# Count-matrix builder of a graph network: one-hots stored with the eight items in the last dimension, and ScalarE fetching slot numbers four at a time

## The reference

```python
def gin_conv(x, W, b, src, dst):
    agg = jax.ops.segment_sum(x[src], dst, num_segments=N)
    return (x + agg) @ W + b
```

## Time and profile before

| | us |
|---|---|
| median of 3 runs | 10942.0 |
| lowest and highest run | 10923.65, 10950.61 |
| the profiled execution | 10955.16 |
| its span | 10953.4 |
| the stage `count_pairs` in it, first DVE step to last ACT step | 3632.6 to 5558.7 |

### The profile page before, as it was taken

How to read it: one execution, slowest core, us unless ns; L and a number is a source line. 1 busy time by engine, 2 the same in 40 slices (tenths; PEclk the granted TensorE clock), 3 DMA queues, 4 the chain that set the end, 5 groups by cost and what they waited for, 6 DMA issues and landing times. The chain is left out here.

```text
span 10953.4 us, 166923 instructions
## 1 busy us (share of the span) xinstructions
PE 6082.3 (56%) x43186; PEld 5047.6 (46%) x43187; DVE 5266.2 (48%) x9074; ACT 2226.6 (20%) x4530; POOL 3602.8 (33%) x3345
## 2 busy tenths in 40 slices
PE   0123333333331556665147766777778778877696
PEld 0122333333331211111046766677777777777496
DVE  6666333333331799998133455233333333333344
ACT  0464000000000344444410000111111111111132
POOL 0001777777776000000000000344545545444100
PEclk9999999999999756665577888788898989898697
DMA  0200222222221222222154755222222222222263
GB/s 21 100 0 9 40 41 41 40 40 40 41 41 26 42 52 52 52 52 52 51 213 159 280 219 213 79 75 73 77 75 75 76 74 76 75 75 74 39 221 119
DMA packets 1450866, 876.35 MB, mean 80 GB/s; under 512 B 905023, under 2 KB 1376596, under 8 KB 1425535
## 3 DMA queue, kind: packets, MB, share of 16 engines
q1 hardware_dynamic: 1237570, 639.77, 20.4%
q0 software_dynamic: 106048, 137.48, 6.0%
q10 hardware_dynamic: 107136, 97.57, 2.5%
HBM read 713.06 MB, written 159.27 MB: 80 GB/s over the span
## 5 line engine op out<-in xcount | busy, mean ns | idle before, releaser
L653 POOL DMA_INDIRECT out_records<-scatter_recs,scatter_rows x1650 | 1958.9, 1187 | 1194.7 <-issue 1194.1
L1567 POOL DMA_INDIRECT edge_mlp_b_rows<-b_table,edge_mlp_recs x1664 | 1633.5, 982 | 2130.7 <-DMA edge_mlp_recs<-out_records 1626.1
L712 PE MATMUL scatter_sum<-scatter_attr,scatter_hot 128*128 128x65 f32 x3328 | 810.5, 422 | 1503.3 <-DMA scatter_attr<-in_edge_attr 1258.2
L712 PEld LDWEIGHTS scatter_sum<-scatter_attr,scatter_hot 128*128 128x128 f32 x3328 | 741.2, 328 | 1572.7 <-DMA scatter_attr<-in_edge_attr 1131.6
L1027 PE MATMUL pairs_p_ring<-pairs_hot_near,pairs_hot_far 128*128 128x512 f16 x2256 | 956.5, 575 | 726.2 <-ACT pairs_p_ring L1046 635.1
L1010 DVE TENSOR_TENSOR pairs_hot_near<-c_iota_wide,pairs_shift 128x4096 f16<-128x4096 f16 x282 | 1244.8, 4414 | 0.0
L1682 DVE CAST edge_mlp_hot_t<-edge_mlp_p_hot 128x512 f32<-128x512 bf16 x416 | 287.6, 691 | 1844.7 <-PE edge_mlp_p_hot L1611 1307.9
L1027 PEld LDWEIGHTS pairs_p_ring<-pairs_hot_near,pairs_hot_far 128*128 128x128 bf16 x2256 | 276.3, 122 | 1406.0 <-issue 1370.7
L760 DVE TENSOR_TENSOR nodes_wide_sums<-nodes_wide_sums,scatter_sum 128x65 f32 x1664 | 384.8, 231 | 1008.2 <-issue 857.2
L1621 PE MATMUL edge_mlp_p_pre<-edge_mlp_hot_t,edge_mlp_a_blk 128*128 128x128 f32 x3328 | 726.5, 303 | 197.8 <-DVE edge_mlp_hot_t L1682 145.6
L1104 POOL MEMSET sum_x_parts<- 128x192 bf16 x2 | 0.5, 260 | 2444.1 <-POOLq L123 2444.1
(11 more groups left out here) (419 smaller groups left out, 9559.0 us busy)
## 6 DMA issues: line engine op xcount, KB each, us to landing
sum_x_tiles<-edge_counts SPq DMA_DIRECT2D x78, 1536.0 KB, 7.6
edge_mlp_a_blk<-a_table SPq DMA_DIRECT2D x1664, 64.0 KB
edge_counts<-pairs_cells ACTq DMA_DIRECT2D x744, 128.0 KB, 1.7
sum_z_tiles<-edge_counts SPq DMA_DIRECT2D x48, 1920.0 KB, 7.8
sum_y_tiles<-edge_counts SPq DMA_DIRECT2D x39, 1536.0 KB, 7.7
scatter_attr<-in_edge_attr SPq DMA_DIRECT2D x1664, 32.0 KB
sum_x_tiles<-edge_counts SPq DMA_DIRECT2D x26, 1664.0 KB, 9.9
pairs_ends<-out_records SPq DMA_DIRECT2D x2256, 1.0 KB, 1.6
```

The lines of the kernel that those rows point to most:

```text
L653: pool.indirect_dma_start(out=out_rec, out_offset=bass.IndirectOffsetOnAxis(ap=rows[s][:, c:c + 1], axis=0), in_=recs[s][:, c], in_offset= ...
L712: mm = pe.matmul(psum[s][:, c, 0:F + 1], hot[s][:, c], attr[s][:, c], start=True, stop=True)
L1567: pool.indirect_dma_start(out=b_rows[s][:, c], out_offset=None, in_=b_tab, in_offset=bass.IndirectOffsetOnAxis(ap=recs[s][:, c, FE + 1:FE ...
```

## The change

The two constant rows are made eight times as long, each number standing eight times in a row. The one-hots are laid out with the eight items innermost: `hot_far[s]` is now `[P, P, BATCH]`, `hot_near[s]` `[P, SUPER, BATCH]`. The comparisons read the long constant row as it lies, and on the other side the eight numbers of the batch again and again, with step 1 within the eight. The number for `hot_far` gets a small bf16 buffer of its own, `low`, with an instruction that fills it; both comparisons stand behind a wait for `shift` and `low`. PE reads item `c` of a batch as `[:, :, c]`, so that neighbouring columns of both operands lie 8 elements (16 bytes) apart. ACT fetches `until`, `plane` and `cell` for four slots at a time.

```diff
-            nc.gpsimd.iota(k["iota_b"][:], [[1, P]], base=0, channel_multiplier=0,
+            nc.gpsimd.iota(k["iota_b"][:], [[1, P], [0, BATCH]], base=0, channel_multiplier=0,
...
-            nc.gpsimd.iota(k["iota_wide"][:], [[1, SUPER]], base=0, channel_multiplier=0,
+            nc.gpsimd.iota(k["iota_wide"][:], [[1, SUPER], [0, BATCH]], base=0, channel_multiplier=0,
...
-        hot_far = [sb(f"hot_far{s}", [P, BATCH, P], BF16) for s in range(BATCHES)]
-        hot_near = [sb(f"hot_near{s}", [P, BATCH, SUPER], FP16) for s in range(BATCHES)]
+        low = [sb(f"low{s}", [P, BATCH], BF16) for s in range(BATCHES)]
+        hot_far = [sb(f"hot_far{s}", [P, P, BATCH], BF16) for s in range(BATCHES)]
+        hot_near = [sb(f"hot_near{s}", [P, SUPER, BATCH], FP16) for s in range(BATCHES)]
...
+        def slots_row(engine, name, it, s, low, top, why):
+            _, values = nc.values_load_multi_w_load_instructions(
+                rows[name][0:1, ds(it * RING + s, HALF)], engines=[engine], min_val=low, max_val=top,
+                skip_runtime_bounds_check_because=why)
+            return values
...
-                    low = ends[s][:].bitcast(BF16)[:, :, 1]
-                    dve.tensor_tensor(hot_far[s][:], bc(k["iota_b"][:], 1, BATCH), bc(low, 2, P),
+                    dve.tensor_copy(low[s][:], ends[s][:, :, 0]).then_inc(shifted[s], 1)
+                    dve.wait_ge(shifted[s], it * 2 + 2)
+                    dve.tensor_tensor(hot_far[s][:], k["iota_b"][:], bc(low[s][:], 1, P),
                                       ALU.is_equal).then_inc(hots_made[s], 1)
-                    dve.wait_ge(shifted[s], it + 1)
-                    dve.tensor_tensor(hot_near[s][:], bc(k["iota_wide"][:], 1, BATCH), bc(shift[s][:], 2, SUPER),
+                    dve.tensor_tensor(hot_near[s][:], k["iota_wide"][:], bc(shift[s][:], 1, SUPER),
                                       ALU.is_equal).then_inc(hots_made[s], 1)
...
-                            pe.matmul(p_ring[:, ds(banks[c], 1), :], hot_far[s][:, c], hot_near[s][:, c], start=False, stop=True,
+                            pe.matmul(p_ring[:, ds(banks[c], 1), :], hot_far[s][:, :, c], hot_near[s][:, :, c], start=False, stop=True,
...
-                    until = nc.values_load(rows["until"][0:1, at], engines=[ACTIVATION], min_val=1, max_val=ITEMS,
-                                           skip_runtime_bounds_check_because="how many items end the slot")
...
-                    act.wait_ge(done, until)
+                    if s % HALF == 0:
+                        until = slots_row(ACTIVATION, "until", it, s, 1, ITEMS, "how many items end the slot")
+                        plane = slots_row(ACTIVATION, "plane", it, s, 0, PLANES - 1, "a plane of the table")
+                        cell = slots_row(ACTIVATION, "cell", it, s, 0, NB - 1, "a block of the plane")
+                    act.wait_ge(done, until[s % HALF])
```

More of the change, by code:

```diff
@@ L57 @@
 BATCHES = 3
+HALF = 4
 CELL_SLOTS = -(-(CELLS + EXTRAS) // RING) * RING
@@ L719, in alloc_constants @@
     k = {n: ctx.enter_context(nc.sbuf_tensor("c_" + n, s, F32)) for n, s in shapes.items()}
-    k["iota_b"] = ctx.enter_context(nc.sbuf_tensor("c_iota_b", [P, P], BF16))
-    k["iota_wide"] = ctx.enter_context(nc.sbuf_tensor("c_iota_wide", [P, SUPER], FP16))
+    k["iota_b"] = ctx.enter_context(nc.sbuf_tensor("c_iota_b", [P, P, BATCH], BF16))
+    k["iota_wide"] = ctx.enter_context(nc.sbuf_tensor("c_iota_wide", [P, SUPER, BATCH], FP16))
     for n, w in (("blk_out", CHUNKS), ("unsorted", 1), ("extra_far", P), ("extra_near", P)):
@@ L1034, in _ @@
                 for s in range(RING):
-                    at = ds(it * RING + s, 1)
-                    until = nc.values_load(rows["until"][0:1, at], engines=[ACTIVATION], min_val=1, max_val=ITEMS,
-                                           skip_runtime_bounds_check_because="how many items end the slot")
-                    plane = nc.values_load(rows["plane"][0:1, at], engines=[ACTIVATION], min_val=0, max_val=PLANES - 1,
-                                           skip_runtime_bounds_check_because="a plane of the table")
-                    cell = nc.values_load(rows["cell"][0:1, at], engines=[ACTIVATION], min_val=0, max_val=NB - 1,
-                                          skip_runtime_bounds_check_because="a block of the plane")
-                    act.wait_ge(done, until)
+                    if s % HALF == 0:
[3 more added lines that the diff above has]
+                    act.wait_ge(done, until[s % HALF])
                     wait_count(act, stored[s], it * 16)
@@ L1046, in _ @@
                     act.mul(p_ring[:, s], p_ring[:, s], 0.0).then_inc(evicted, 1)
-                    act.dma_start(planes[:, ds(plane, 1), ds(cell, 1)], cells[s][:].unsqueeze(1).unsqueeze(1)).then_inc(stored[s], 16)
+                    act.dma_start(planes[:, ds(plane[s % HALF], 1), ds(cell[s % HALF], 1)], cells[s][:].unsqueeze(1).unsqueeze(1)).then_inc(stored[s], 16)
             for s in range(RING):
```

## The result

| | before | after |
|---|---|---|
| time, median of 4 runs each, same chip | 10932.96 us (10923.65 to 10950.61) | 11245.33 us (11220.63 to 11250.61) |
| span of the profiled execution | 10953.4 us | 11248.9 us |
| stage of the count matrix: first matmul to PE's last end | 3638.5 to 5278.7, 1640 us | 3649.7 to 5695.6, 2046 us |
| ACT's slots behind it | 280.1 us | 172.6 us |

The changed kernel takes 1.0279 times as long, interval [1.0257, 1.0301]: 2.8% slower. I had said 2.0% slower; the measured time lies within the forecast case's own range, 10940 to 11390, and not only within the wide one, 10250 to 11430, which holds faster outcomes too.

The account below looks back on a forecast made before the run. ACT was taken to bound the kernel, DVE hard beside it, PE with slack. Profiled 10955.2 + 323 - 102 - 2 + 4 = 11178 us; on the median 10942 + 223 = 11165, 2.0% slower, range 10250 to 11430.

Parts of the forecast that it names:

- the forecast case: PE's strided matmuls pace the count-matrix stage at 0.87 us each: 11165 us, own range 10940 to 11390, chance 0.48.
- ACT's fetches: Twelve fetches per four slots become three; slot 1.63 us instead of 2.58, tail of 109 slots -102 us.
- DVE's comparisons: With step 1 on 16-bit operands, two elements at a time: hot_near 2.40 us, hot_far 0.71, 3.6 us per batch.
- PE's operands: Columns 16 bytes apart cost 1.50 to 1.90 ns each by `place_out`; 0.87 us per matmul, +323 us in the item-paced piece.
- The first batch: DVE's first batch at the start of the stage is ready about 2 us sooner: -2 us.
- The constants: Constant rows at the program's start grow by 896 and 3584 elements at 0.83 ns: +4 us.
- Cover: In the item-paced piece DVE (3.6 us a batch), ACT (1035 us) and SP's issues stay under PE's 7.0 us a batch.
- The next stage: It begins behind a tail with PE idle, as before, so its clock starts alike; no time term.
- Rival 1: Strided reading costs PE nothing or hardly; ACT stays the bound, stage 1275 us, total 10303; no penalty, chance 0.30.
- The intermediate rival: Strided reading costs PE about 0.6 us per matmul: total 10556 us, chance 0.12.
- the rival without DVE's gain: DVE keeps one element at a time and PE pays nothing: 10926 us, no change, chance 0.05.
- the worse one: Moving operand 0.97 us with weights in sequence, 1.16 us per matmul: total 11819 us, chance 0.05.

Follow-up runs that it names:

- experiment 1: Kernel before with only ACT's fetches for four slots at a time, old one-hot layout: 9696.98 us against 9876.92, ratio 0.9821.
- experiment 5: Changed kernel with only the moving operand hot_near 16 bytes apart, weights contiguous: 11159.6 us against 10888.11 for the kernel before, one run.
- experiment 6: Changed kernel with only the weights hot_far 16 bytes apart, moving operand contiguous: 10621.85 us against 10888.11 for the kernel before, one run.
- experiment 3: Changed kernel with four items innermost in two groups, columns 8 bytes apart: 9579.76 us against 9876.92 for the kernel before, ratio 0.97.
- experiment 4: Changed kernel with two items innermost in four groups, columns 4 bytes apart: 9573.47 us against 9876.92 for the kernel before, ratio 0.9695.
- experiments 2: Changed kernel with ACT's single fetches put back, so the layout alone: 10310.82 us against 9876.92 for the kernel before, ratio 1.044.
- experiment 8: Changed kernel with PE reading the same bytes contiguously, counts of wrong columns: 10584.6 us against 10888.11 for the kernel before, one run.
- experiments 9 and 10: Kernel with two items innermost, half of SP's loads issued by POOL: 10188.19 us; instead one load per batch: 10183.77; kernel before 10897.49.
- experiment 7: Changed kernel with PE reading 256, 256 and 128 columns at steps of 16, 32 and 64 bytes: 10627.84 us, -260, one run.

## Why the prediction was right, step by step

- *What bounds the kernel* (ACT by itself, DVE hard beside it, PE with slack): right. With ACT relieved alone DVE is 100% busy (experiment 1).
- *ACT's fetches*, -102 us from 1.63 us a slot: measured -107.5. The slot is 1.63 us in the mean as said: the covered ones 1.25 (1.27 said), the first of four 2.57 and 2.99 in turn (2.7 said). Of the 5.5 us, 4.9 are three slots fewer in the tail; that ACT keeps level with a slower PE is the likely reason. Three fetches of four numbers end 1.42 or 1.83 us after the DMA issue, three fetches of one number 1.36: 0.47 or 0.61 us for a fetch of four against 0.45 for a fetch of one.
- *DVE's comparisons* at two elements at a time: hot_near 2.285 us (2.40 said), hot_far 0.693 (0.71 said). The step of zero innermost was what held them to one (experiments 5 and 6). Experiments 3 and 4 add that inner rows of four or of two elements keep the rate: 2284 and 2285 ns. There was luck in the size: 0.55 ns per element came from a one-input instruction on fp32, and nothing said that two inputs of 16 bits would run at the same rate. An estimate from the figure of the Trainium skill, "VectorE: DVE Perf Modes", section "The perf-mode tier table" (1224 ns for 2048 elements), was 2.3 us; the trace now agrees, 2.285.
- *PE's operands*, the step that decided: +323 us forecast, +406 measured. The mechanism is right, by experiments 2, 5 and 8; the term was mis-sized, at 0.87 us per matmul where it is 0.906, 1.77 ns per column. I took the middle of two readings of `place_out`; the one that gave all the time to the moving operand (1.90) was the nearer one, and the one that let the weights share it (1.50) was wrong by its assumption, as experiment 6 shows. So it is partly luck that the middle came so near: one reading was too high and the other too low. The remark that a rise of the clock does not help is right. The changed kernel alone can't show it, since 1.00 was granted in all of its stage; experiment 3 does, with bursts of 3.80 us at 0.50 and at 1.00. The prediction also calls the 0.422 us of the first burst the time at the lower clock. In the kernel before, the burst from 3654.99 to 3658.58 was granted 0.50 and took the same 3.59 us, so the price stands, but in that first burst itself 1.00 was granted.
- *The first batch*, -2 us: -2.0.
- *The constants*, +4 us: +8.5. The step that failed is the 0.83 ns per element, taken from a contiguous row; with eight equal numbers in a row POOL needs 1.80.
- *Cover*: DVE, ACT and SP under PE's 7 us a batch: right for the changed kernel, SP by 5.1 against 7.25. For SP the prediction gave no number.
- *The next stage*, whose clock was said to start alike: it did not. In a window of 30 us that begins 11 us behind `count_pairs` the granted clock was 0.74 before and is 1.00 after; PE is busy 19 of the 30 us either way, and no gain shows.
- *The sum*: +223 us on the median forecast, +312 measured. Of the 73 us between forecast and the spans' 295.5, 83 are in PE's term, -5.5 in the tail, 4.5 in the constants, and -9 in stages that nobody touched.
- *Rival 1*, no penalty, 10303: it did not happen, and its price was wrong as well. It counted PE, DVE and ACT, and left out the fourth worker of the stage, SP. Its rows were at hand: eight issues 0.5 us apart and a fetch, some 5 us a batch, against the (1275 - 172) / 282 = 3.9 us that the rival's items would take. Without the penalty and with SP as it is, the gain is 300 us (experiment 8); the rival's figure comes only with SP relieved (experiments 9 and 10).
- *The intermediate rival*, 0.6 us per matmul, falls by 0.906 measured; the rival without DVE's gain by 2285 ns; the worse one, with the weights in sequence, by experiment 6.
- The Trainium skill, "SBUF — State Buffer", section "Specifications (TRN2)", was right to speak against the change. Its line of 16 bytes agrees with experiment 7, in which 16, 32 and 64 bytes cost 1.79 to 1.86 ns per column. Its rule that two hits per line give full bandwidth does not fit PE at the higher clock: with two columns per line a matmul takes 0.452 us (experiment 3, granted 1.00), with four 0.24 (experiment 4). The measurement decides.

What stays open: why 16 bytes cost 1.77 ns. No run separates the reading of a line from its way to PE. Experiments 5 to 8 and the one with a single load are one run each; their readings rest on the traces.

## What to carry to other kernels

Before you turn a layout round to make one engine faster, price the other reader: for PE's moving operand of 16-bit numbers keep four columns within 16 bytes, which cost nothing here, while DVE already has its double rate with two elements innermost. When you price what happens if the first bound goes, list every queue that does something per batch, those that only issue DMAs too, in us per batch; the one forgotten here was worth 390 us, the items' 1440 against 1050. Then put part of its issues on an engine that is idle.

## What the runs showed of the hardware

- PE's moving operand, 2-byte columns: 1.77 to 1.79 ns per column at a step of 16 bytes, 1.82 at 32, 1.86 at 64; 0.88 at 8 bytes; nothing beyond the contiguous time at 4. With 16 bytes this was so at a granted clock of 1.00, with 8 bytes at 0.50 and at 1.00. A step of 16 bytes in the weights costs next to nothing behind 512 columns: 0.907 us against 0.901 behind a strided moving operand, 0.22 to 0.24 behind a contiguous one, though the load itself lasts 146 ns instead of 128 (medians of the changed kernel and of experiment 5).
- DVE compares two 16-bit inputs of 128 x 4096 elements in 2285 ns if the innermost dimension has 2, 4 or 8 elements at step 1, with a step of zero outside it; with a step of zero innermost it takes 4414.
- In the kernel before, the stage's granted clock was 0.61 in the mean; with the slow matmuls, which keep PE busy without a break, it is 1.00, and a matmul still takes 0.906 us, where contiguous ones take 0.23 at that level.
- POOL writes a row of numbers at 1.80 ns per element with each number eight times in a row, and at 0.83 with each once.
- SP issues DMAs with fetched addresses 0.52 us apart though each issue lasts 0.33; POOL's issue lasts 0.534, and four of them take 2.31 us. Beside the 1128 of POOL an issue of SP still lasts 0.333.
